# Two attentions of a megakernel: pairs attended by twos, full-height similarities, and the last key's score without TensorE

## The reference

```python
h = token_mixer(x)                      # AFT-style mixing with exp(k), exp(w_bias), layer norm -> [32, 256, 256]
h = concat([cls_tok, h], axis=1)        # 257 rows, the class row first
# first attention: 16 heads, 16 wide keys, 64 wide values
q, k, v = l2norm(q), l2norm(k), l2norm(v)
attn = square(relu(q @ k.T))            # no softmax
h = h + tanh_norm(attn @ v) @ Wout
# second ("latent") attention: 16 heads, 16 wide, causal softmax over 257 rows
scores = where(causal, q @ k.T / 4, -1e9);  a = softmax(scores)
h = h + layernorm(h) + ((a @ v) @ Wo)   # written short: the block adds to its own input
# mixture of 8 experts, top 2, hidden width 512, silu
h = h + moe(rmsnorm(h))
```

## Time and profile before

| what | value |
|---|---|
| median of three runs | 3332.42 us (3327.59 to 3339.62) |
| the profiled execution's own time | 3334.22 us |
| its span, first to last instruction | 3332.5 us |
| busy time of TensorE, VectorE, ScalarE, GpSimd | 3075.5, 2038.0, 1413.8, 1095.9 us |
| share of the span | 92%, 61%, 42%, 33% |
| mean granted TensorE clock | 0.961 |
| data moved over the span | 223.15 MB, 67 GB/s |

### The profile page before, as it was taken

One profiled execution on the slowest core, in us unless ns is written; L12 is line 12 of the kernel. 1 busy time (PEld: TensorE's weight loads), 2 busy tenths in 40 slices (PEclk: granted clock), 3 DMA queues, 4 the chain that ended last, 5 costly groups with the idle time before them and its releaser, 6 DMA issues. The chain is left out here.

```text
span 3332.5 us, 69096 instructions
## 1 busy us (share of the span) xinstructions
PE 3075.5 (92%) x22960; PEld 2320.1 (70%) x22961; DVE 2038.0 (61%) x5211; ACT 1413.8 (42%) x2884; POOL 1095.9 (33%) x965
## 2 busy tenths in 40 slices
PE   3999999999999999999859999999999980899998
PEld 1677777777777777777537777777777760799997
DVE  4667767776776777677425666666666654344444
ACT  0444454454445445444314444444444432344443
POOL 3333443343244334334211222222222221344444
PEclk7999999999999999999869999999999995899999
DMA  3342343244234324423100001001001005454444
GB/s 80 89 102 64 87 101 85 69 98 101 68 84 101 85 69 98 98 61 93 48 18 18 34 30 38 32 31 38 32 32 36 31 31 152 71 77 76 76 78 69
DMA packets 160728, 223.15 MB, mean 67 GB/s; under 512 B 30033, under 2 KB 125202, under 8 KB 160674
## 3 DMA queue, kind: packets, MB, share of 16 engines
q1 hardware_dynamic: 134738, 187.50, 22.3%
q0 software_dynamic: 25936, 34.95, 6.7%
HBM read 125.26 MB, written 97.08 MB: 67 GB/s over the span
## 5 line engine op out<-in xcount | busy, mean ns | idle before, releaser
L657 ACT ACTIVATE R<-psA 128x1024 f32<-128x1024 f32 x256 | 263.0, 1027 | 149.4 <-PE psA L1143 146.7
L849 DVE TENSOR_TENSOR PR<-R 128x1024 f32<-128x1024 f32 x256 | 321.8, 1257 | 0.0
L66 POOL TENSOR_TENSOR vrn<-vsm,inv_root 128x16 f32<-128x16 f32 x64 | 214.5, 3352 | 320.0 <-DVE vsm L828 320.0
L1869 DVE TENSOR_REDUCE m_nm<-psC 128x4 f32<-128x516 f32 (+1 forms) x256 | 239.5, 958 | 130.9 <-PE psC L2141 130.2
L2489 POOL DMA_INDIRECT out_rows<-e_y,e_dest x137 | 212.2, 1549 | 322.4 <-DMA out_rows<-e_y,e_dest 208.5
L1158 PE MATMUL psA<-PR,V 128*64 128x258 f32 x2048 | 285.8, 400 | 0.0
L662 ACT ACTIVATE oTs<-psA 128x258 f32<-128x258 f32 x256 | 98.8, 386 | 411.9 <-PE psA L1158 409.8
L1740 ACT ACTIVATE m_PT<-psC 128x770 f32<-128x770 f32 x256 | 197.7, 799 | 154.9 <-PE psC L2170 154.9
L1203 PE MATMUL psA<-wout,OT 128*128 128x256 f32 x1024 | 259.2, 397 | 0.4 <-DVE OT L891 0.4
L1657 POOL DMA_INDIRECT xg<-r_tn,r_idx x130 | 127.8, 983 | 358.6 <-DMA xg<-r_tn,r_idx 241.9
L1203 PEld LDWEIGHTS psA<-wout,OT 128*128 128x128 f32 x1024 | 188.8, 194 | 35.7 <-issue 1.1
(11 more groups left out here) (419 smaller groups left out, 7726.9 us busy)
## 6 DMA issues: line engine op xcount, KB each, us to landing
ks<-kparts SPq DMA_DIRECT2D x256, 128.0 KB, 3.3
qs<-qparts SPq DMA_DIRECT2D x256, 128.0 KB, 3.6
e_x<-xg SPq DMA_DIRECT2D x143, 129.0 KB
xraw<-in_x SPq DMA_DIRECT2D x66, 256.0 KB
qparts<-qh SPq DMA_DIRECT2D x128, 128.0 KB, 2.4
kparts<-kh SPq DMA_DIRECT2D x64, 128.0 KB, 2.5
kparts<-kl SPq DMA_DIRECT2D x64, 128.0 KB, 2.4
qparts<-ql SPq DMA_DIRECT2D x64, 128.0 KB, 2.4
```

The source lines that it names most:

```text
L66: return pool.tensor_tensor(out, x, e.to_broadcast(list(out.shape)), ALU.pow)
L657: act.activation(R[:, p % 2], ps[:, 0:2, :].rearrange("p a (t n) -> p a t n", t=LT), ACT.Relu).then_inc(relu_done, 1)
L849: dve.tensor_tensor(PR[:, p % 2, :, :, 0:L], R[:, p % 2], R[:, p % 2], ALU.mult).then_inc(prob_done, 1)
L1869: dve.tensor_reduce(nm[:, t, :, DK], ps[:, 0:4, cols], AX.X, ALU.max, negate=True).then_inc(max_done, 1)
```

## The change

In the first attention:

- `sim` works at full height. `qs` has two copies of the queries, one for each head, with zeros in the 64 rows of the other head, so that one product of 128 rows and 512 columns (two heads of 256) takes the place of two products of 64 rows and 256 columns. `lay_out` becomes `lay_out_keys` and `lay_out_queries`, with as many transfers of the same sizes.
- `attend` takes two pairs: two products for the class token at full shape, then the 64-column products of both pairs. It is called for the pairs 0, 2, 4, 6.
- TensorE's order changes: `sim` runs up to two pairs ahead, `attend(0)` comes behind `mix_values`, `attend(2)` behind `spread_scale` 0 and 1, `attend(4)` behind `project_outputs` 2 and `sim(6)`, `attend(6)` behind `class_products`. ScalarE's order follows. VectorE's stays.
- `spread_scale` uses 80 contraction rows (`ind80`, `scs` of 80 rows).

In the latent attention the last key's score is the element of the first scores (`ps[:, 0:4, L]`) less the maximum. Its exponential multiplies the last value, on every partition, and is added before the division:

```diff
-                pe.matmul(ps[0:4, 3, FREE:FREE + 1], kb[:, d, g, :], qx[:, g % 2, L - 1:L], ...)
-                pe.matmul(ps[:, OB + g % 2, L - 1:L], vc[:, d, g, :], pcT[:, g % 2, :], ...)
+                for t in (1, 0):
+                    ...
+                dve.wait_ge(max_done, LT * n + 1)
+                dve.tensor_tensor(own[:, g], ps[:, 0:4, L], nm[:, 1, :, DK], ALU.add).then_inc(own_done, 1)
```

The maxima are taken and turned in the other order (the 257-column part first), each transposition waits only for its own part, `mask_keys` waits for `own`, and `last_values` writes 128 partitions instead of 4. The core of the rest:

```diff
             def sim(i, p):
                 if p == 0:
+                    pe.wait_ge(other_rows, 2)
                     pe.wait_ge(moved0, 128 * i + 128)
 ...
                 for t in range(LT):
-                    for hh in range(2):
-                        rows = slice(64 * hh, 64 * hh + 64)
-                        last = pe.matmul(ps[:, hh, t * L:(t + 1) * L], ks[rows, p, t * P:(t + 1) * P], qs[rows, p, :],
-                                         start=True, stop=True, skip_group_check=True)
+                    last = pe.matmul(ps[:, t, :].rearrange("p (a n) -> p a n", a=2), ks[:, p, t * P:(t + 1) * P],
+                                     qs[:, :, p, :], start=True, stop=True, skip_group_check=True)
-            def attend(i, d, p):
+            def attend(i, d, first):
+                pairs = (first, first + 1)
 ...
+                need(pe, o_sq, PAIRS * i + first)
+                for p in pairs:
+                    pe.matmul(ps[:, 2 + p % 2, 0:QCOLS], v.vcls3[:, p * P:(p + 1) * P], v.pcl[:, d, :], ...)
+                for p in pairs:
+                    pe.wait_ge(prob_done, PAIRS * i + p + 1)
+                    for t in range(LT):
+                        for hh in range(2):
 ...
                 sim(i, 1)
-                attend(i, d, 0)
                 if more:
                     mix_keys(j)
                 sim(i, 2)
                 if more:
                     mix_values(j)
-                attend(i, d, 1)
+                attend(i, d, 0)
                 if more:
                     residual(j)
                 sim(i, 3)
-                attend(i, d, 2)
                 if before:
                     turn_scale(i - 1, more)
 ...
-                attend(i, d, 3)
+                attend(i, d, 2)
                 sim(i, 5)
 ...
+                sim(i, 6)
                 attend(i, d, 4)
 ...
                     project_queries(j)
-                    project_values(j, 0)
-                sim(i, 6)
-                if more:
-                    project_values(j, 1)
-                attend(i, d, 5)
                 sim(i, 7)
                 if more:
+                    project_values(j, 0)
+                    project_values(j, 1)
                     key_sums(j)
 ...
                 attend(i, d, 6)
                 if more:
                     query_sums(j)
-                attend(i, d, 7)
```

`divide` of the latent attention, before and after its first steps:

```diff
-                dve.reciprocal(rec[:, g % 2], out[:, :, :, DK]).then_inc(rec_done, 1)
+                dve.wait_ge(own_exp, n + 1)
+                dve.tensor_tensor(add[:, g % 2, 1], vlast[:, d, 4 * g:4 * g + 4],
+                                  ownp[:, g].unsqueeze(2).to_broadcast([P, 4, DK + 1]), ALU.mult).then_inc(add_done, 1)
+                dve.wait_ge(back_done, n + 1)
+                dve.wait_ge(add_done, n + 1)
+                dve.tensor_tensor(ow[:, g % 2], out, add[:, g % 2], ALU.add).then_inc(ow_done, 1)
+                dve.wait_ge(ow_done, n + 1)
+                dve.reciprocal(rec[:, g % 2], ow[:, g % 2, :, :, DK]).then_inc(rec_done, 1)
```

More of the change, by code:

```diff
@@ L880, in split_scale @@
             def split_scale(i):
-                turned = ps[0:48, BSC, 0:L]
+                turned = ps[0:CROWS, BSC, 0:L]
                 dve.wait_ge(sc_turned, i + 1)
@@ L1689, in _ @@
             pool.memset(both[:], 0.0).then_inc(preset, 1)
-            pool.memset(own[:], 0.0).then_inc(preset, 1)
-            pool.wait_ge(preset, 7)
-            pool.affine_select(out=own[:], in_=own[:], compare_op=ALU.not_equal, fill=1.0, base=0,
-                               pattern=[[0, GROUPS], [-1, 4]], channel_multiplier=1).then_inc(preset, 1)
+            pool.memset(vlast[:, :, :, DK:DK + 1], 1.0).then_inc(preset, 1)
+            pool.memset(add[:], 0.0).then_inc(preset, 1)
             pool.memset(zrow[:], 0.0).then_inc(pad_done, 1)
@@ L1970, in sample @@
                 if before:
-                    divide(i - 1, 2)
-                    divide(i - 1, 3)
+                    divide(i - 1, e, 2)
+                    divide(i - 1, e, 3)
                 if behind:
@@ L1990, in sample @@
                     choose(i)
-                divide(i, 0)
+                divide(i, d, 0)
                 maxima(i, 3)
                 lower_queries(i, d, 3)
-                divide(i, 1)
-                if behind:
-                    last_key(j, e)
+                divide(i, d, 1)
                 if behind == 2:
@@ L2004, in last @@
                 norm_tokens(i + 1, d, x)
-                divide(i, 2)
-                divide(i, 3)
+                divide(i, d, 2)
+                divide(i, d, 3)
                 give_slots(i + 1, 1 - d)
@@ L2023, in _ @@
             normalise(0, 0)
-            dve.wait_ge(preset, 8)
+            dve.wait_ge(preset, 6)
             class_keys(0, 0)
@@ L2131, in scores @@
                     if h % 2 == 0:
-                        need(pe, exp_done, 3 * n - 2 + h)
+                        need(pe, exp_done, 2 * n - 1 + h // 2)
                     if h == 0 and first:
@@ L2146, in turn_maxima @@
                 n = 4 * i + g
-                pe.wait_ge(max_done, LT * n + LT)
                 need(pe, o_copied, n - 1)
-                for t in range(LT):
+                for t in (1, 0):
+                    pe.wait_ge(max_done, LT * n + LT - t)
                     last = pe.transpose(ps[:, OB + g % 2, L + t * P:L + (t + 1) * P],
```

182 lines of the change are left out of this document (87 added, 95 removed).

## The result

The changed kernel takes 3363.4 us (median of 4 runs, 3360.4 to 3370.7), the kernel before 3333.4 beside it on the same chip: ratio 1.0093, with a 95% interval of 1.0068 to 1.0118. The forecast was 3366.

A forecast was written before the change was run, and what follows sets the result against it. TensorE was taken to set the pace, with a transfer chain to sim(0) barely hidden behind it. Loop +30, clock +42, earlier falls -5, latent attention -34, rest -1 gave +32 on 3334.2: 3366 us, range 3318 to 3394.

The forecast's parts named there:

- (a): First attention, sim(0) to mixer_output: 15.44 us becomes 15.0, with 1.6 of TensorE idle time waiting for VectorE.
- (b): First attention, mixer_output to the end of the low keys: 19.3 us becomes 20.8, no wait added.
- (c): First attention, low keys to next sim(0): 13.77 us becomes 13.7; TensorE ready at 11.5 waits 2.1 for the queries' transfers.
- The clock: First attention at sim(0): the wait drops the clock to half in nine of ten samples, 1.55 us each, +42 us.
- The price of a tile shape: TensorE in the first attention: 0.18 us per change of tile shape, 25 fewer changes, 4.5 us less a sample.
- Loop and clock: First attention's 30 steady samples: +30 us for the longer loop, +42 for clock falls, -5 for falls already there before.
- The signs named: First attention: waits at sim(0) and mixer_output, TensorE busy near 0.92, clock 0.93 to 0.97; latent sample 1 us shorter.
- The latent attention: Last-key products go, first maxima are turned earlier: 1.1 us less in each of 31 samples, -34 us.
- The rest: Zeroing of qs, relu's order, split_scale, constants' load and GpSimd's presets: together -1 us, bounds -2 to +1.
- the first (clock holds, 3324): Rival: the wait at sim(0) is there but the clock does not fall, -10 us, 3324 us; chance 0.18.
- The second (loads in time): Rival: the queries' loads land by 11.5 us after the low keys, no wait at sim(0), 3258 us; chance 0.09.
- The third (two falls): Rival: a second clock fall in each sample, behind the waits at mixer_output, 3406 us; chance 0.13.

The follow-up runs named there:

- prob2_later: The changed kernel with only VectorE's prob(2) moved behind mixed_rows: 3289.6 us, ratio 0.9869 to the kernel before.
- half_loads: The changed kernel without two of ten stores, the rows they fed loaded by two 16-row loads instead of one of 32: 3330.9 us, ratio 0.9997 to before.
- old_order: The changed kernel with the earlier TensorE and ScalarE order and one pair per visit; full-height similarities and 80-row spread products stay: 3267.3 us, ratio 0.9807 to before.
- latent_only: The changed kernel with the first attention of the kernel before, so only the rest is changed: 3291.2 us, ratio 0.9889 to before.
- first_only: The changed kernel with the latent attention of the kernel before: 3394.8 us, ratio 1.0203 to before.
- products_in_wait: The changed kernel with seven idle 512-column products ahead of the wait of sim(0) in every sample: 3309.1 us, ratio 0.9947 to before.
- work_in_wait: The changed kernel with mixer_queries and the previous sample's head_sums issued ahead of sim(0) instead of behind it: 3286.7 us, ratio 0.9876 to before.
- wiw_prob2_later: The changed kernel with mixer_queries and head_sums ahead of sim(0), and VectorE's prob(2) behind mixed_rows: 3258.7 us, ratio 0.9781 to before.
- single_visits: The changed kernel with mixer_queries and head_sums ahead of sim(0), prob(2) behind mixed_rows, two more shape changes in each of four visits: 3280.8 us, ratio 0.9840 to before.
- best_half: The changed kernel with head_sums, then mixer_queries ahead of sim(0), sums_out ahead of relu(0), prob(2) behind mixed_rows, half-size loads: 3242.2 us, ratio 0.9730 to before.

## Why the prediction was right, and where it was not

- **(a) sim(0) to mixer_output**, 15.0: 14.98 in the sample without a fall. TensorE alone was put at 13.4 and the wait at 1.6; prob2_later has 13.3 and 1.65, of which the profile shows 1.2 as idle time ahead of `osc`. Its cause, prob(2) in VectorE's chain, was shown by moving it.
- **(b)**, 20.8: 20.97, without a wait in it; TensorE had a little more to do than counted.
- **(c)**, 13.7 with TensorE ready at 11.5: 13.57, ready at 11.55. The wait was put at 2.1 and is 1.9. That SyncE's issues make it was shown by taking two away, and by half_loads with the same bytes.
- **The clock**: a fall of 1.55 in nine of ten samples; it was 29 of 30, and 1.58 by the one sample without (in prob2_later 13.3 without and mostly 14.8 or 14.9 with one stretch of 3.4 us). That the idle time makes these falls was shown by the seven products, 29 to 0. It isn't the only cause: before had 4 and old_order 6 without idle time there, as the prediction had seen once. That the length of the gap alone decides was refuted by prob2_later. No fall followed the wait at mixer_output in this kernel, as forecast.
- **The price of a tile shape**: 0.18, measured 0.175 for 64-column products.
- **Loop and clock** together +67, measured +72. The signs named fit: TensorE is busy 0.94 of the first attention (0.92 was named) at a clock of 0.97.
- **The latent attention**: -34, measured -27 here and -32 in latent_only between the first and the last maxima. Groups 2 and 3 gain 0.23 each from their maxima to the next group's, made of the earlier turning (0.12) and the absent last key (0.12), where I had 0.29. For group 1 I had 0.05, because its maxima would wait for the longer divide. They do, but by 0.11 only: in the median sample they start 0.18 after the last score product ended, 0.07 in the kernel before. Even so the way from group 0's maxima to them is 0.22 shorter and the way on to group 2's 0.22 (0.34 in latent_only). The 0.14 for last_values and the exponential don't show.
- **The rest**, -1: measured -17. This is the term that failed. I summed 30 steady samples and took the last one at nothing, but it has no next sample's work beside it, and went from 71.3 to 61.2 us; TensorE was busy 49.3 of them before and 40.6 after. old_order, with full height and 18 changes of shape fewer, took 65.1 us for it at a granted clock of 0.83 (0.76 before, 0.79 changed), busy 43.1: so part of the 10 us comes with the full height, in time or in clock, and 4 with the order and the pairs. The way to the first maxima gained 3.5 more. It took 20.4 us before and 20.0 in first_only, at clocks of 0.61 and 0.62, and 16.9 to 17.0 at 0.76 to 0.79 in all twelve runs with the changed latent attention, so it belongs to that half; which of its edits does it is open. Of the 16 us from the last sample to the first maxima latent_only has 6 and first_only 11.
- So the sum (+32 for +28 in the traces) is as near as it is because errors of +5, +7 and -16 stand against each other, and that is luck. The sign did not depend on it.
- **Rivals**: the first (clock holds, 3324) is what products_in_wait built, -0.5% where it had -0.2%, the term of the rest again. The second (loads in time) never came by itself; its condition, a landing by 11.5 us, fits the 11.55 at which TensorE was ready. The third (two falls) didn't happen.

## What to carry to other kernels

When TensorE is made faster in a loop that a transfer chain just fits into, compute when each stretch's other input arrives: the saving beyond that point becomes a wait, and a wait may cost the clock on top. Look for work that is ready at the place of the wait and stands behind it only by order; moving two calls was worth 69 us, 2.1%, in the steady samples here. And test the parts of a change apart: full height with the old order and the latent part gave 1.9% less time, hidden in a change that gave 0.9% more.

## What was unexpected in the hardware

- Idle time in front of sim(0) and samples at half clock, in one execution each: 0.6 us 3 of 30, 1.25 us 19, 1.87 us 29, but 1.92 us only 15 in prob2_later. Without idle time there 4 of 30 (before), 6 (old_order) and 3 (latent_only) had one, and none in work_in_wait, wiw_prob2_later, single_visits and best_half.
- A load of 16 rows costs SyncE the same as one of 32, 0.46 us (2.73 for six, four of them with 16 rows; 1.89 for four with 32).
- The latent attention takes 30.44 us a sample in seven of these runs and 30.6 to 30.7 in the five others, with the same code; that is 6 us of the time. The difference lies between group 1's maxima and group 2's, 9.06 us in the seven and 9.18 to 9.24 in the five; its cause is open.
